# Unit-matrix products put into TensorE's waits in the norms and the routers of an eight-layer kernel

## The reference

```python
    x = L0_attn_tokens
    x = _layernorm(x + _L0_attn_ref(x, ...), axis=-1)   # recurrent mixer, 256 steps
    x = _layernorm(x + _L0_ffn_ref(x, ...), axis=-1)    # 8 experts, top 2, softmax weights
    x = _layernorm(x + _L1_attn_ref(x, ...), axis=-1)   # latent attention
    x = _layernorm(x + _L1_ffn_ref(x, ...), axis=-1)    # 64 gated experts, top 6 of 4 groups
    x = _layernorm(x + _L2_attn_ref(x, ...), axis=-1)   # gated linear attention
    x = _layernorm(x + _L2_ffn_ref(x, ...), axis=-1)    # 160 experts, top 8
    x = _layernorm(x + _L3_attn_ref(x, ...), axis=-1)
    x = _layernorm(x + _L3_ffn_ref(x, ...), axis=-1)
    return x

def _layernorm(x, axis=-1, eps=1e-05):
    m = jnp.mean(x, axis=axis, keepdims=True)
    v = jnp.var(x, axis=axis, keepdims=True)
    return (x - m) / jnp.sqrt(v + eps)
```

## Time and profile before

| What | us |
|---|---|
| median of 3 runs | 1920.63 |
| lowest and highest run | 1919.22 and 1922.42 |
| span of the profiled execution | 1914.6 |
| PE busy / DVE busy / ACT busy | 1691.7 / 1499.7 / 1262.2 |
| mean granted clock of TensorE over the span | 0.883 of full speed |

### The profile page before, as it was taken

One profiled execution on the slowest core, in us unless ns is written; L12 is line 12 of the kernel. 1 busy time (PEld: TensorE's weight loads), 2 busy tenths in 40 slices (PEclk: granted clock), 3 DMA queues, 4 the chain that ended last, 5 costly groups with the idle time before them and its releaser, 6 DMA issues. The chain is left out here.

```text
span 1914.6 us, 45800 instructions
## 1 busy us (share of the span) xinstructions
PE 1691.7 (88%) x16657; PEld 1055.0 (55%) x16662; DVE 1499.7 (78%) x3630; ACT 1262.2 (66%) x3371; POOL 453.8 (24%) x581
## 2 busy tenths in 40 slices
PE   5999977969869999966679999999969999999786
PEld 4999973437634444444444444444436666566453
DVE  4444457968779999978779999999967877788675
ACT  5666646856646655567558888888856666566675
POOL 1000001318411111110012222222214344435333
PEclk7555568969979999978789999999979999999998
DMA  3200005500024444200056666666610000000000
GB/s 80 91 4 4 4 13 196 190 1 2 2 98 157 156 163 169 106 1 1 1 206 234 224 222 231 233 226 222 230 61 23 12 11 23 23 2 1 1 11 15
DMA packets 52464, 174.80 MB, mean 91 GB/s; under 512 B 7376, under 2 KB 32976, under 8 KB 34896
## 3 DMA queue, kind: packets, MB, share of 16 engines
q1 hardware_dynamic: 51152, 170.69, 24.8%
q10 hardware_dynamic: 1152, 1.90, 0.3%
HBM read 168.05 MB, written 2.95 MB: 89 GB/s over the span
## 5 line engine op out<-in xcount | busy, mean ns | idle before, releaser
L864 DVE TENSOR_TENSOR ps<-ps,m_comb 128x512 f32<-128x512 f32 x520 | 363.0, 698 | 24.7 <-DMA m_comb<-m_shares 7.4
L849 DVE TENSOR_TENSOR m_hwlo<-ps,m_hwhi 128x512 f16<-128x512 f32 x520 | 353.6, 680 | 0.3
L825 ACT ACTIVATE m_hwhi<-ps 128x512 f16<-128x512 f32 x520 | 308.7, 594 | 20.9 <-DVE ps L864 19.5
L831 ACT ACTIVATE ps<-ps 128x512 f32<-128x512 f32 x388 | 225.8, 582 | 80.5 <-PE ps L781 80.4
L754 POOL CAST m_whi<-m_stage 128x256 f16<-128x256 f32 (+1 forms) x130 | 55.5, 427 | 899.9 <-PE ps L787 633.6
L781 PE MATMUL ps<-x_hi,m_whi 128*128 128x512 f16 x652 | 249.3, 382 | 11.1 <-DVE m_hwlo L849 6.6
L781 PE MATMUL ps<-x_lo,m_whi 128*128 128x512 f16 x652 | 249.1, 382 | 0.0
L781 PE MATMUL ps<-x_hi,m_wlo 128*128 128x512 f16 x652 | 248.9, 382 | 0.0
L463 DVE TENSOR_TENSOR rn_s_lo<-rn_s_full,rn_s_hi 128x32 f16<-128x32 f32 x512 | 98.5, 192 | 131.8 <-ACT rn_s_full L420 131.8
L787 PE MATMUL ps<-m_hwhi,m_whi 128*128 128x512 f16 x520 | 197.5, 380 | 0.3 <-DVE m_hwlo L849 0.2
L787 PE MATMUL ps<-m_hwlo,m_whi 128*128 128x512 f16 x520 | 197.3, 379 | 0.0
(11 more groups left out here) (456 smaller groups left out, 3973.2 us busy)
## 6 DMA issues: line engine op xcount, KB each, us to landing
m_comb<-m_shares SPq DMA_DIRECT2D x128, 1024.0 KB, 5.1
m_stage<-in_m_w SPq DMA_DIRECT2D x97, 128.0 KB, 4.5
m_stage<-in_m_w SPq DMA_DIRECT2D x33, 192.0 KB, 4.6
kept_lj_w<-in_lj_w SPq DMA_DIRECT2D x6, 1024.0 KB, 4.9
kept_lq_w<-in_lq_w SPq DMA_DIRECT2D x1, 1600.0 KB, 8.0
kept_la_w<-in_la_w SPq DMA_DIRECT2D x1, 1280.0 KB, 5.6
rn_rows<-in_L_attn_rows SPq DMA_DIRECT2D x4, 256.0 KB, 4.3
rn_xs<-rn_xn_hi SPq DMA_DIRECT2D x32, 32.0 KB, 1.9
```

The source lines that it names most:

```text
L825: nc.scalar.activation(hw_hi[:, k % HB, :], weighted(k), ACT.Copy).then_inc(hi_done, 1)
L831: nc.scalar.activation(acted(k), ps[:, 4, :] if gated else bank(k), func).then_inc(act_done, 1)
L849: nc.vector.tensor_tensor(hw_lo[:, k % HB, :], weighted(k), hw_hi[:, k % HB, :], ALU.subtract)\
L864: nc.vector.tensor_tensor(weighted(k), bank(k), comb[:, s, n * QW:(n + 1) * QW], ALU.mult)\
```

## The change

A new helper, `exercise`, issues a number of bf16 products of the unit matrix with itself repeated four times, 128 x 512, into one PSUM bank. Nothing reads the result, they wait for nothing and signal nothing. They go to bank 7, in three places of TensorE's list of each norm and in one of each router: 8 behind `turn_in`, 3 behind the first and 3 behind the second `turn_back`, and 24 between `seed` and the wait for the first half's shares. That is 5 x 14 + 3 x 24 = 142 products. Nothing is removed and no other engine's list changes.

```diff
+def exercise(nc, S, bank, times):
+
+    for _ in range(times):
+        nc.tensor.matmul(S.psum[:, bank, :], S.identb[:], S.identb[:].unsqueeze(1).broadcast_to([P, 4, P]), start=True,
+                         stop=True, skip_group_check=True)
...
             for g in range(G):
                 turn_in(g)
-            for g in ORDER:
+            exercise(nc, S, 7, 8)
+            for n, g in enumerate(ORDER):
                 turn_back(g)
+                if n < 2:
+                    exercise(nc, S, 7, 3)
...
         pe.wait_ge(self.score_s, NT // 2)
         seed()
+        exercise(nc, self.S, 7, 24)
         for n, (h, c, q) in enumerate(self.turns):
             cols = self.chunks[c]
             pe.wait_ge(self.scaled, h + 1)
```

## The result

| | before | with the change |
|---|---|---|
| median of 11 runs, us | 1918.36 | 1924.77 |
| lowest and highest, us | 1915.45 and 1922.42 | 1919.79 and 1927.90 |
| ratio of the runs, 95% interval | | 1.003, 1.0019 to 1.0040 |
| span of the profiled execution, us | 1914.6 | 1918.0 |

The change makes the kernel slower by 0.3%, 3.6 to 7.7 us. The forecast was 1922.4 us, +1.8 us, in a range from 1916.5 to 1926.5: the time is inside it, the sign is right, and the loss is some three times as large. The case "slower by over 0.2%", which had 19%, is the one that came. That the forecast time looks as near as it does is partly luck: the median of the kernel before went from 1920.63 us (3 runs) to 1918.36 us (11 runs), and these 2.3 us hide part of the miss in the change.

The account below looks back on a forecast made before the run. It took the VectorE and ScalarE chain to bound the norms, and TensorE the first products behind them. Router 0 +2.6, behind norms -1.2, router 2 +0.4 sum to +1.8 us on 1920.6: 1922.4 us, range 1916.5 to 1926.5.

Parts of the forecast that it names:

- slower by over 0.2%: Whole kernel over 1924.5 us: products at half clock in router 0 (14%) or norms lengthened by the products (5%); chance 19%.
- The norms neutral: Inside each norm the products fit TensorE's idle time and slack: 0 us, bounds 0 and +1 us per norm.
- Router 0 a loss by the run length of the products: Router 0: 24 products outlast the wait for shares, transposes start 2.7 us late: +2.6 us, bounds +2.3 and +2.8.
- The rival with the clock: Router 0: products run at half clock, sum +7.2 us; with a late rise +3 to +5; 14% for over +3.9 us.
- The credits of -1.2 us: Behind the norms, full clock lasts 0.6 us into the next stage: -0.6 us each in l1_attn and router 2.
- Router 1 nothing: Router 1: the 24 products end 2 us before the first half's shares: 0 us, bounds 0 and -0.9 us.
- Router 2 +0.4: Router 2: faster first transposes, longer idle, second half may run at half clock: +0.4 us, bounds -0.2 and +1.7.

## Why the prediction was right, and where it was wrong

**The norms neutral: right.** 13.04 to 13.42 us against 13.02 to 13.42 (in the other profiles with empty gaps one norm took 13.66 us and no other over 13.44), and the norms alone cost nothing that can be measured (0.9993).

**Router 0 a loss by the run length of the products: right in kind.** The sum had +2.6 us; three traces with 24 products in router 0 have +2.7. It is also where the loss is, as far as it can be measured: with router 0 left out the rest measures 1.0001, with 8 products there 1.0001, with 48 it is 1.0044. What was mis-sized is its bound. The bounds of +2.3 and +2.8 us took the seed's end from one trace. Over the ten profiles with empty gaps the seed of router 0 took 5.1 to 6.7 us, and it ended 12.3 to 13.9 us after the first score product, before 12.4. Without the products the wait hides such a delay (1.4 us in the trace of all but router 0); with them it is paid: +2.7 in three traces and +4.2 in another. The rival with the clock named this as a case by itself, with +3 to +5 us, and tied it to the products running at half clock. They ran at full clock in every trace; the seed was what was slow.

**The credits of -1.2 us: mostly wrong.** The step that failed is the one from two norms of before, dense up to their end and with 0.5 and 0.7 us of full clock left, to 0.6 us at every site. With the products the last transposes are themselves faster and end earlier, so the idle stretch grows: 3.87 us ahead of router 0 where it was 3.23, and 4.15 us ahead of l1_attn where it was 3.50. Whether that is the reason isn't shown, since what was left behind such stretches went from nothing to 1.4 us. In the first trace l1_attn starts at half clock and router 2 gets 0.2 us. Over the profiles with the norms' products and empty gaps, l1_attn started at full clock in three of six, for 0.2 to 1.0 us, and then took 109.2 to 109.4 us instead of 109.87; in the other three it took 109.9 to 110.1. So the term is -0.5 us in some executions and 0 or +0.2 in others; I had taken it at nearly its full bound. I had also overlooked GpSimd there, 4.24 us busy in the very window that I cited the earlier trace rows.

**Router 1 nothing: right in the first trace** (26.98 against 26.96). In three later ones with the norms' products it took 26.4 to 26.5 us: there full clock lasted 1.2 to 1.4 us into its scores.

**Router 2 +0.4: the mechanism was wrong.** The first transposes took 1.97 us instead of 3.67 and the second batch fell back to half clock, 3.68 us, as described, but from the first transpose to the experts it is the same 11.43 us as before. ScalarE's copies and stores covered it. Yet over the six traces with 24 products there and empty gaps the whole stretch is 27.5 to 29.1 us, against 27.6 to 27.8 in four without. Two of the six have the scores' clock rise later (7.7 us from scores to seed instead of 6.9), and two have a slow issue of two stores on ScalarE's queue, here in the kernel with 8 products in router 0 and, for comparison, with the change:

```profile
984.55 1.88 ACTq L575 DMA_DIRECT2D m_shares<-m2r_combT  x2
```

```profile
987.87 0.84 ACTq L575 DMA_DIRECT2D m_shares<-m2r_combT  x2
```

That these three traces (28.5, 28.7 and 29.1 us) all have products in router 2 may be chance; no run has products in router 2 alone.

**The sum.** Without the credits and router 2's term, and with the late seed in its bounds, it would have been +2.6 to +4.2 us. The measured ratios are 1.0030 and 1.0025 for the change (+5.8 and +4.8 us) and 1.0013 and 1.0020 for router 0's products without the norms' (+2.5 and +3.8 us). The intervals overlap, and the norms alone measure -1.3. In the trace of the second measurement of the change router 0 has +4.2 us of a span that is 5.5 us over before, and router 2 and the experts of l0_ffn have +0.8 us each. Whether the full change costs another 1 to 2 us beside router 0 stays open.

## What to carry to other kernels

A wait of an engine in one trace is not free room: it also absorbs what varies from run to run, here a seed that is 1.3 us longer when the clock rises late. Filler should end before the earliest moment at which its engine can be wanted, also where it or the work ahead of it runs at the slower clock: in router 1 twelve products at half clock took 4.01 us and held up the transposes. To keep the clock, filler has to stand in the last idle stretch ahead of dense work, and it pays only where the next engine waits for that work: here some 2 us of 1918 in all, and that only just clear of the noise.

## What the runs showed of the hardware

Where TensorE idled for 3.1 to 4.2 us between a norm and the next stage, full clock was gone at the stage's start or at most 1.4 us after it, in every trace. With 12 products in that stretch 1.2 to 1.6 us of idle time were left; then the scores of router 2 and the first 5 us of both attention stages ran at 1.00, while the 64-column scores of router 1 lost full clock 1.7 us after their start and the 8-column scores of router 0 2.7 and 3.5 us after theirs. In the trace with 3.5 us PE was busy from their start at 281.68 to the end of this window (3.22 us), and PEld too:

```profile
281.00:284.90 3.90, 3.22 (x29) 3.25 (x30) 0.45 (x3) 1.10 (x6) 0.00 (x0) 1.00 0.28 69
```

A second thing. The first stage, up to the first norm at 269 us, runs at half clock for most of its length in some executions and at full in others. It made no difference to its length: the first norm starts at 268.6 to 271.0 us in nine traces of the first kind and at 268.6 to 270.6 us in four of the second. The slices of the change's first trace and of the one taken again are these.

```profile
PEclk7555568979979999988889999999979999999998
```

```profile
PEclk9999998989979999998889999999979999999899
```
